# Turning the normalised context by a transposing DMA in place of TensorE transposes, in a fused gated cross-attention and FFN kernel

## What is computed

```
q_hk = (hidden_q @ Wq.T).reshape(Bv, Sv, H, K)
q_big = jnp.einsum('bshk,hkq->bshq', q_hk, w_kc_q)
...
q_r = jnp.einsum('bshq,hqr->bhsr', q_big, W_qr)
k_r = jnp.einsum('bld,hdr->bhlr', kv_r, W_kr)
scores = jnp.einsum('bhsr,bhlr->bhsl', q_r, k_r)
attn = jax.nn.softmax(scores, axis=-1)
ctx_c = jnp.einsum('bhsl,bld->bhsd', attn, kv_r)
ctx_lat = jnp.einsum('bhsd,hkd->bhsk', ctx_c, w_kc_kv)
ctx = ctx_lat.transpose(0, 2, 1, 3).reshape(Bv, Sv, H * K)
return ctx @ Wo.T
```

## Time and profile before

| | |
|---|---|
| median of 3 runs | 487.31 us (487.01 to 488.1) |
| the profiled execution | 489.46 us, its span 487.6 us |
| busy share PE / DVE / ACT / POOL | 86 / 77 / 58 / 53 % |
| stretch of the loop over the groups | about 142 to 345 us of the span |

### The profile page before, as it was taken

One profiled execution on the slowest core, in us unless ns is written; L12 is line 12 of the kernel. 1 busy time (PEld: TensorE's weight loads), 2 busy tenths in 40 slices (PEclk: granted clock), 3 DMA queues, 4 the chain that ended last, 5 costly groups with the idle time before them and its releaser, 6 DMA issues.

```text
span 487.6 us, 11500 instructions
## 1 busy us (share of the span) xinstructions
PE 418.3 (86%) x4416; PEld 313.0 (64%) x4416; DVE 377.1 (77%) x757; ACT 283.0 (58%) x640; POOL 257.7 (53%) x293
## 2 busy tenths in 40 slices
PE   2975898798967879989987898888879899999994
PEld 2445466346846756767665666666767678887773
DVE  4359998676668979886989999985765689888991
ACT  1677587775346666556655756646515456567660
POOL 3168131201345545546678777764353488888373
PEclk9997799999989999999999999987989999999998
DMA  8994003930124666668666745488211476777643
GB/s 258 268 340 105 0 2 99 367 125 1 60 69 92 129 108 131 121 105 146 113 111 149 138 80 85 78 184 177 52 47 54 116 194 174 190 174 214 192 50 34
DMA packets 104599, 62.60 MB, mean 128 GB/s; under 512 B 72032, under 2 KB 100704, under 8 KB 104352
## 3 DMA queue, kind: packets, MB, share of 16 engines
q1 hardware_dynamic: 99792, 56.69, 47.9%
q0 software_dynamic: 4224, 4.79, 5.8%
q10 hardware_dynamic: 528, 0.38, 0.4%
HBM read 40.27 MB, written 8.55 MB: 100 GB/s over the span
## 4 chain that ended last, share of the span: by engine, by line
PE 42%; DMA 16%; DVE 13%; ACT 10%; POOL 8%; issue 7%; SPq 1%; POOLq 0%; DVEq 0%; ACTq 0%
PE psum L2179 7%; DMA lw<-lw 6%; PE psum L1871 5%; PE psum L2195 4%; DMA y_sb<-lw 4%; DVE lw L1296 4%; ACT lw L965 3%; DMA out_x<-lw,tslot 3%; POOL out_x L753 3%; PE psum L1992 2%; PE psum L1796 2%; PE psum L1956 2%; DVE nmax L1353 2%; POOL lw L651 2%; PE psum L1938 2%
## 5 line engine op out<-in xcount | busy, mean ns | idle before, releaser
L651 POOL TENSOR_TENSOR lw<-lw 128x512 f32<-128x512 f32 x48 | 67.3, 1404 | 53.7 <-DVE lw L1296 53.6
L965 ACT ACTIVATE lw<-psum,nmax 128x256 f32<-128x256 f32 x128 | 59.0, 469 | 33.3 <-DVE nmax L1353 31.6
L1871 PE MATMUL psum<-lp 128*128 128x256 f16 x576 | 72.1, 276 | 0.0
L1296 DVE TENSOR_TENSOR lw<-psum,lp 128x1024 f32<-128x1024 f32 x48 | 58.4, 1218 | 7.8 <-PE psum L1871 6.8
L1871 PEld LDWEIGHTS psum<-lp 128*128 128x128 f16 x576 | 53.6, 99 | 14.0 <-issue 7.4
L1077 ACT ACTIVATE lw<-psum,b1w 128x320 f16<-128x320 f32 x64 | 33.7, 527 | 36.9 <-PE psum L2179 36.9
L2179 PE MATMUL psum<-lw,se 128*128 128x320 f16 x384 | 54.7, 299 | 0.0
L753 POOL DMA_INDIRECT out_x<-lw,tslot x24 | 43.8, 1827 | 18.2 <-DMA out_x<-lw,tslot 7.3
L972 ACT ACTIVATE lw<-lw 128x512 f16<-128x512 f32 x60 | 37.6, 630 | 27.0 <-DMA lw<-lw 19.8
L712 POOL TENSOR_TENSOR lw<-lw 128x512 f16<-128x512 f32 x30 | 35.6, 1187 | 30.8 <-ACT lw L972 30.8
L2179 PEld LDWEIGHTS psum<-lw,se 128*128 128x128 f16 x384 | 36.3, 97 | 16.6 <-DVE lw L1598 1.3
(11 more groups left out here) (248 smaller groups left out, 986.8 us busy)
## 6 DMA issues: line engine op xcount, KB each, us to landing
se<-in_w SPq DMA_DIRECT2D x11, 1024.0 KB
se<-in_w SPq DMA_DIRECT2D x40, 128.0 KB
dispatch<-in_empty SPq DMA_DIRECT2D x4, 662.5 KB, 9.3
lp<-in_Wq SPq DMA_DIRECT2D x2, 1024.0 KB, 9.7
se<-in_WoT SPq DMA_DIRECT2D x1, 2048.0 KB, 12.2
lw<-dispatch SPq DMA_DIRECT2D x7, 265.0 KB, 7.3
lp<-in_w_kc_q SPq DMA_DIRECT2D x2, 768.0 KB, 10.0
lp<-in_rotq SPq DMA_DIRECT2D x1, 1536.0 KB, 13.9
```

The source lines that it names most:

```text
L651: nc.gpsimd.tensor_tensor(rope[:, c % QT, :].rearrange("p (h s) -> p h s", h=2), straight, crossed[:, ::-1, :], ALU.add).then_inc(g_rope, 1)
L965: A_(e_sb[:, n % 2, st * S:(st + 1) * S], bank[3 + n % 2][:, st * S:(st + 1) * S], ACT.Exp, bias=nmax[:, n % 2, st:st + 1], accum_out=esum ...
L1296: V.tensor_tensor(t12[:, c % 2], tile_bank(c).unsqueeze(1).broadcast_to([P, 2, 2 * S]), rotq[:, c % QT], ALU.mult).then_inc(v_t1, 1)
L1871: ins = M(tile_bank(c)[:, half * S:(half + 1) * S], m1[w][:, kc, half, col:col + P], (yth, ytl)[a][:, kc, b * S:(b + 1) * S], start=(n == ...
```

## The change

For groups 0 to 13 the context is turned by SP's transposing DMA. ACT now writes the fp16 high half straight from `cxn` (`context_high`, at the place of `ct_high`), POOL the low half (`ct_low`, now on POOL), both into a free part of `y_sb`, and SP turns the two together into `ct` (`turned_context`). `project` waits for that DMA. PE's four transposes and DVE's subtraction go away for these groups; groups 14 and 15 keep the old way. Some semaphores of the routing steps are replaced by the wait chain `link`.

```diff
+NGD = NGB - 2
...
+            def turned_context(g):
+
+                sp.wait_ge(g_ct, g + 1)
+                if g >= 1:
+                    sp.wait_ge(p_out, g)
+                sp.dma_start_transpose(ct.rearrange("p w st a s -> p (w st a) s"), context_halves(g)).then_inc(d_ct, 16)
...
             for n in range(NHD):
                 turned_exps(n)
+                if n % G == 1 and n > G:
+                    turned_context(n // G - 1)
...
+            def ct_low(g):
+
+                pool.wait_ge(a_ct, g + 1)
+                halves = context_halves(g)
+                nc.gpsimd.tensor_tensor(halves[:, 512:1024], cxn, halves[:, 0:512], ALU.subtract).then_inc(g_ct, 1)
...
                 exps_low(n + 1)
+                if g >= 1:
+                    ct_low(g - 1)
                 if g + 2 < NGB:
                     rotate(QT * (g + 2))
                 exps_low(n + 3)
...
+            def context_high(g):
+
+                act.wait_ge(v_norm, g + 1)
+                if g >= 1:
+                    act.wait_ge(d_ct, 16 * g)
+                A_(context_halves(g)[:, 0:512], cxn, ACT.Copy).then_inc(a_ct, 1)
...
                 exps(n + 3)
                 if g >= 1:
-                    ct_high(g - 1)
+                    context_high(g - 1)
...
                 if g + 2 < NGB:
                     turn(QT * (g + 2) + 1)
-                if g >= 1:
-                    ct_low(g - 1)
...
             def project(g):
 
                 b = g // NG
-                pe.wait_ge(v_ct, g + 1)
+                if g < NGD:
+                    pe.wait_ge(d_ct, 16 * (g + 1))
+                else:
+                    pe.wait_ge(v_ct, g - NGD + 1)
...
                     queries(QT * (g + 2) + 1)
-                if g >= 1:
-                    turn_context(g - 1)
```

More of the change, by code:

```diff
@@ L158, in program @@
         cxn = w2([512])
-        ct = [w2([512], F16) for _ in range(2)]
+        ct = w2([1024], F16).rearrange("p (w st a s) -> p w st a s", w=2, st=TPB, a=2)
         nmax = sb("nmax", [P, 2, TPB])
@@ L302, in program @@
         s_y3, g_row, p_yT3, a_yT3, p_lg = sem("s_y3"), sem("g_row"), sem("p_yT3"), sem("a_yT3"), sem("p_lg")
-        g_nb, v_best, v_cnt, s_rows = sem("g_nb"), sem("v_best"), sem("v_cnt"), sem("s_rows")
-        v_sel, d_sel, s_base = sem("v_sel"), sem("d_sel"), sem("s_base")
+        g_nb, v_cnt, s_rows = sem("g_nb"), sem("v_cnt"), sem("s_rows")
+        v_sel, d_sel = sem("v_sel"), sem("d_sel")
+        g_ct, d_ct = sem("g_ct"), sem("d_ct")
         s_el, a_el, s_oh, p_pos, s_idx, v_meta = sem("s_el"), sem("a_el"), sem("s_oh"), sem("p_pos"), sem("s_idx"), sem("v_meta")
@@ L350, in turn_bank, with context_halves @@
             return (bank[5], bank[1])[n % 2]
+        def context_halves(g):
+            at = NT - 2 * TPB if g < (B - 1) * NG - 2 else 0
+            return y_sb[:, at:at + TPB, :].rearrange("p a b -> p (a b)").bitcast(F16)
         def context_bank(g):
@@ L978, in turned_high @@
                 A_(turned[n % 3][:, 0].rearrange("p st lt s -> p (st lt s)"), turn_bank(n)[:, :], ACT.Copy).then_inc(a_at, 1)
+            def context_high(g):
[3 more added lines that the diff above has]
+                A_(context_halves(g)[:, 0:512], cxn, ACT.Copy).then_inc(a_ct, 1)
             def ct_high(g):
-                act.wait_ge(p_ct, g + 1)
-                if g >= 1:
-                    act.wait_ge(p_out, g)
-                A_(ct[0], context_bank(g)[:, :], ACT.Copy).then_inc(a_ct, 1)
+                act.wait_ge(p_ct, g - NGD + 1)
+                act.wait_ge(p_out, g)
+                A_(ct[:, 0].rearrange("p st a s -> p (st a s)"), context_bank(g)[:, :], ACT.Copy).then_inc(a_ct, 1)
             def split_high(k):
@@ L1374, in norm @@
                 dve.wait_ge(p_cx, G * (g + 1))
-                if g >= 1:
-                    dve.wait_ge(p_ct, g)
+                if g > NGD:
+                    dve.wait_ge(p_ct, g - NGD)
+                elif g >= 1:
+                    dve.wait_ge(g_ct, g)
                 V.tensor_tensor(cxn.rearrange("p (a b) -> p a b", b=DC),
@@ L1382, in ct_low @@
                 dve.wait_ge(a_ct, g + 1)
-                V.tensor_tensor(ct[1], context_bank(g)[:, :], ct[0], ALU.subtract).then_inc(v_ct, 1)
+                high, low = [ct[:, w].rearrange("p st a s -> p (st a s)") for w in range(2)]
+                V.tensor_tensor(low, context_bank(g)[:, :], high, ALU.subtract).then_inc(v_ct, 1)
             def update(b):
@@ L1420, in route_best @@
                 for t, l in zip(ts, lg):
-                    V.max_index(i8[:, t, :], v8[:, t, :], l).then_inc(v_best, 1)
+                    ins = V.max_index(i8[:, t, :], v8[:, t, :], l)
+                link(ins)
             def route_choice(b):
                 ts = pair_of(b)
-                dve.wait_ge(v_best, TPB * (b + 1))
                 link(V.tensor_copy(idf[:, ts, :], i8[:, ts, 0:TOPK]))
@@ L1438, in route_sides @@
                                 ALU.subtract).then_inc(s_el, 1)
-                V.tensor_scalar(base[:, ts, :], idf[:, ts, :], float(CAP), spare[:, 0:1], ALU.mult, ALU.subtract)\
-                    .then_inc(s_base, 1)
+                link(V.tensor_scalar(base[:, ts, :], idf[:, ts, :], float(CAP), spare[:, 0:1], ALU.mult, ALU.subtract))
             def route_weights(b):
@@ L1475, in route_place @@
                 dve.wait_ge(v_cnt, 2 * b + 2)
-                dve.wait_ge(s_base, b + 1)
                 link(V.tensor_reduce(pos[:, ts, :], pr[:, ts, :, :], AX.X, ALU.add))
@@ L1923, in latent @@
                     pe.wait_ge(v_qz, g)
-                if g >= 3:
-                    pe.wait_ge(v_ct, g - 2)
                 x, y = bank[1], bank[2]
@@ L1999, in turn_context @@
                 pe.wait_ge(v_norm, g + 1)
-                pe.wait_ge(v_qz, min(g + 3, NGB))
+                pe.wait_ge(v_qz, NGB)
                 if g == NGB - 1:
@@ L2004, in turn_context @@
                     for pair in range(2):
-                        ins = TR(context_bank(g)[:, pair * S + st * P:pair * S + (st + 1) * P],
+                        ins = TR(context_bank(g)[:, (2 * st + pair) * P:(2 * st + pair + 1) * P],
                                  cxn[:, st * S + pair * P:st * S + (pair + 1) * P], identf[:, :])
@@ L2019, in project @@
                             last = g % NG == NG - 1 and pair == 1 and (a, w) == PASSES[-1]
-                            ins = M(bank[7][:, st * S:(st + 1) * S], ct[a][:, pair * S + st * P:pair * S + (st + 1) * P],
+                            ins = M(bank[7][:, st * S:(st + 1) * S], ct[:, a, st, pair, :],
                                     nn[w][:, 2 * (g % NG) + pair, :], start=(first and st == 0), stop=last,
@@ L2114, in select_rows @@
                     pe.wait_ge(v_t1, QT * NGB)
-                    pe.wait_ge(v_ct, NGB - 1)
+                    pe.wait_ge(v_ct, 1)
                 for t in (TPB * b, TPB * b + 1):
```

## The result

| | before | after |
|---|---|---|
| median | 487.16 us (4 runs) | 510.8 us (508.27 to 513.56, 4 runs) |
| ratio, 95% interval | | 1.0495 (1.0447 to 1.0544) |
| profiled execution, its span | 489.46, 487.6 us | 508.27, 506.5 us |

The changed kernel's lines are other ones: `project` is L2050, `context` L2019, `scores` L1983, `latent` L1958; on ACT `context_high` is L1009, `exps_high` L996; on POOL the new `ct_low` is L735, `rotate` L667, `exps_low` L728; on SP the context's DMA is L528, a head's DMA L484.

A forecast was written before the change was run, and what follows sets the result against it. No engine is full; a ring of waits through POOL's and SP's lists bounds the loop. Six passes at 1.5, four at 1.0 (4.0) and four at 0.4 (1.6) add 14.6 us to 487.31: 501.9 us, range 494 to 507.

The forecast's parts named there:

- Pass 4: Loop pass worked out by rows: SP issues the context, weight pieces and late heads 18 and 19; next `latent` +1.7 us.
- Passes 6, 10, 11, 12: Loop passes taken to be like pass 10, without weight pieces on SP; +1.0 us each, 4.0 together.
- Passes 5, 8, 9, 13: Loop passes taken to be like pass 5, with tight DVE or POOL's scatters; +0.4 us each, 1.6 together.
- first class: Loop passes 1, 2, 3, 4, 7, 14, like pass 4 with weight pieces on SP's list; +1.5 us each.
- last class: The same as Passes 5, 8, 9, 13: loop passes with tight DVE or POOL's scatters; +0.4 us each.
- The deeper one: Rival, 20%: `project` has its full delay in every pass, 14 x 1.9 = 26.6 us, 513.9; also covers a blocked port.
- The blocked port: Within the deeper rival: DVE and POOL operations reading SBUF lengthen each other when they meet, up to 1.1 us each.
- The faster one: Rival, 9%: PE's own list sets the passes, so its 9.2 us saving comes back nearly whole; 479.
- The hidden one: Rival, 5%: delays of heads n+2 and n+3 fall into idle time and PE's savings pay the rest; 487.3.
- The colder PE: Rival, 8%: longer gaps lower PE's granted clock; one 12 us slice at half clock costs about 10 us; 512.
- the 7 us that I had held ready: Upper allowance for the new DMA landing in 4.6 instead of 3.1 us in passes with high DMA share: 5 x 1.5.
- the ring: Loop's waits across engines taken to set each pass: DVE `turn`, POOL `rotate` and `exps_low`, head's DMA, PE `context`, next `latent`.

The follow-up runs named there:

- d3_spare_both: Kernel before plus an unused POOL subtraction and an unused transposing DMA waiting for it, at the change's places; 512.92 us, 1.0514.
- d4_both_behind: As d3_spare_both, with the spare DMA moved in SP's list from behind head n+1 to behind head n+3; 493.32 us, 1.0145.
- e4_high_early: The change with ACT's `context_high` moved ahead, right behind `qz_high` instead of behind head n+3's exponentials; 487.38 us, 1.0041 to before.
- f1_early_behind_piece: As e4_high_early, with the context's DMA behind head n+1's weight piece on SP instead of ahead of it; 489.53 us, 1.0071 to before.
- f2_early_first12: As e4_high_early, but groups 12 and 13 keep the old TensorE transposes; 486.92 us, 1.0020 to before.
- q1_not_turned: The change with turning of groups 0 to 13 left out (no transposes, low half or DMA), an incomplete computation; 483.42 us, 0.9945 to before.
- d2_spare_low: Kernel before with the change's `link` waits and an unused POOL subtraction at `ct_low`'s place, nobody waiting for it; 488.99 us, 1.0051.
- d1_spare_turn: Kernel before with the change's `link` waits and one unused transposing DMA per group on SP, waiting for nobody; 490.72 us, 1.0055.
- e1_project_late: The change with PE's `project` moved one pass later, behind the next pass's first queries; 523.98 us, 1.0764 to before.

## Why the prediction held, and where its sum was off

**The mechanism.** Heads n+2 and n+3 queued on SP behind a wait that passes through POOL to ACT: shown by d3_spare_both (1.0514 with nothing else of the change) and undone by either end, d4_both_behind (SP's order) and e4_high_early (ACT's).

**Pass 4.** Forecast +1.7 us, measured +2.36. Counted from each pass's own `latent`, `context_high` and its successors came 0.2 us later than worked out, gaps of 0.1 us between SP's issues another 0.2, and head 19 landed after 3.29 instead of 3.1 us.

**The sum.** From `latent` to `latent`, after less before: passes 1 to 4 and 7, forecast 1.5 each, measured 1.49 on average (2.41, -0.72, 1.78, 2.36, 1.61). Passes 6, 10, 11, 12, forecast 1.0, measured 1.45 (3.29, 2.57, 0.20, -0.27). Passes 5, 8, 9, 13, forecast 0.4, measured 1.32 (0.53, 2.09, 0.77, 1.89). The last is the term that was mis-sized most: 5.3 us in place of 1.6 (pass 14 was in the first class and ends outside the loop).

The 1.49 of the first class agrees by luck. Passes 3, 4 and 7, with the granted clock at 1.00 before and after, grew by 1.9 us on average, and pass 1 had a clock of 0.88 in place of 1.00. Against that stands pass 2: it takes 14.23 us before and 11.7 to 11.8 in e4_high_early, f1_early_behind_piece, f2_early_first12 and q1_not_turned. So the work taken away gives back some 2.5 us there, which the forecast did not have, and the delay ate 1.8 of it.

In the last class passes 5 and 9 came near the forecast, and 8 and 13 did not. I had taken DVE for the tight engine in all four, so that its own 0.68 us would pay. Pass 8 has a colder PE, below. In pass 13 SP issues two weight pieces behind each head and behind the context too; the change there:

```profile
340.96 1.24 SPq L528 DMA_TRANSPOSE lw<-y_sb  x1
342.26 1.05 SPq L473 DMA_DIRECT2D se<-in_w  x2
343.40 1.23 SPq L484 DMA_TRANSPOSE lw<-lw  x1
```

Head 54 is issued 11.3 us after the pass's `latent` at 332.07, where it was 8.9 before, and the pass grows by 1.9 us although its clock rose from 0.89 to 1.00: it is a pass like pass 4, and I had it in the wrong class. DVE is tight in none of them any more. Before, it was busy for 13.49 of pass 9's 14.57 us; after, by this row of the busy time, for 11.66 of 15.34:

```profile
275.37:290.71 15.34, 11.76 (x151) 8.82 (x148) 11.66 (x17) 8.22 (x24) 11.90 (x11) 1.00 0.80 170
```

**The clock.** The forecast had it only in a rival. Pass 6 before; pass 6 and pass 8 after; and a stretch of 4 us at the start of pass 6:

```profile
222.17:234.68 12.51, 12.14 (x160) 9.61 (x157) 9.98 (x20) 8.59 (x26) 7.63 (x9) 1.00 0.68 113
...
229.22:245.02 15.80, 13.51 (x155) 9.91 (x152) 11.26 (x22) 8.75 (x26) 9.35 (x10) 0.89 0.56 111
...
259.69:275.37 15.68, 12.57 (x147) 8.97 (x144) 11.79 (x13) 8.11 (x24) 10.59 (x11) 0.89 0.62 122
...
228.00:232.00 4.00, 3.23 (x32) 1.99 (x34) 1.57 (x4) 2.03 (x6) 1.74 (x4) 0.67 0.91 210
```

PE had been busy for 1.92 of the 4 us from 208, for 2.46 and 2.70 of two of the next three stretches, with a granted clock of 1.00; then 0.67 is a part at 1.2 GHz. `latent` of this pass, which the next steps wait for, took 3.8 us where it had taken 2.15 in pass 6 before at 1.00. So up to 1.65 of the pass's 3.3 us are clock. From pass 1 on the change has three such passes, 1, 6 and 8, and the kernel before one, 13. The four executions of the change took 508.27, 509.97, 511.63 and 513.56 us at a mean clock of 0.969, 0.949, 0.950 and 0.940.

So the forecast's 501.9 is low by 8.9 us. Of these, 4.2 are between its 504.1 for the profiled execution and the 508.27 measured, from the passes and the clock above; 2.2 are the distance by which the profiled execution of before lay above its median, which the forecast carried over; and 2.5 are the distance by which that of the change lay below its own, at the highest clock of the four.

**The rivals.** The deeper one had nearly the right time (513.9) and half of its rows: `project` does wait 1.8 us in every group. But the wait is not the cause: without it, d3_spare_both takes as long. It hides in the same delay: there PE stands at `context` instead, 21.6 us for heads to land (142 to 364 us), where it is 15.2 in the change and 12.1 before. That its time came near the measured one is luck. The blocked port is not seen: the mean of `exps_low` on DVE went from 850 to 742 ns and of `rotate` from 1404 to 1390 ns with one more POOL operation in a group, where the lock that I cited from the Trainium skill's "SBUF — State Buffer" would have them longer; with fewer DVE instructions in a longer pass they may meet less, but in d2_spare_low, with all of DVE's work, the means hardly moved either. The faster one is excluded by q1_not_turned: with PE's 9.2 us and DVE's 9.6 us gone, 2.7 us come back, so PE's own list does not set the passes. The hidden one is excluded by the result. The colder PE has the nearest time, 512, and its clock is there in passes 1, 6 and 8; but it comes on top of the delay in SP's list and not in its place, so its number too is right in part by luck.

**Costs beside the order.** The spare DMA by itself is 0.55% and the spare subtraction 0.51%, 5 us together, about twice what q1_not_turned gives back. The waits of `link`, which I had put at nothing, are in both and are not separated. The landing of the new DMA was like the others: median 3.1, at most 3.7 us, so nothing of the 7 us that I had held ready for it above. Two small slips in the forecast move no bound: 0.60 + 1.2 + 3.1 is 4.9 and not 4.95, and 5 x 1.5 is 7.5 and not 7.

**What stays open.** The share of the 24 us that is clock is not separated by a run. And why e4_high_early loses 1.6 us in pass 12 and 1.5 in pass 13 is half settled. f2_early_first12 has the old way from pass 13 on, for groups 12 and 13, and its pass 13 is as long as before (15.58 against 15.63 us), so the new way costs there. Its pass 12, still with the new way, is 1.5 us longer than before; but so is that of q1_not_turned, by 1.6, which issues no new DMA at all. So SP's list is not the cause in pass 12; what is stays open. Each of these is one profiled execution, and the median of f2_early_first12 is not below that of before.

## What to carry to other kernels

Before moving work to an in-order DMA queue, write down what stands behind it there and when its input is ready: a wait costs whatever is queued behind it, not what it waits for. If the place is given, make the source earlier; here one line on the producer was worth 22 us. And look for the ceiling first, by leaving the work out: 19 us of engine time taken off two busy engines were worth 2.7 us.

## What the runs showed of the hardware

- Transposing DMAs of 128 x 1024 fp16 that wait for no other engine cost a kernel that already issues 60 of them only 0.55% for 14 more (d1_spare_turn), though the DMA share of the loop rose from 0.65 to 0.76.
- The kernels with more waits on PE, of 1 to 3 us each, had the lower granted clock in the loop: 0.97 before, 0.95 in the change, 0.92 in d3_spare_both and, in e1_project_late, by its busy time of 142 to 380 us:

```profile
142.00:380.00 238.00, 187.23 (x2146) 138.72 (x2147) 160.39 (x248) 123.60 (x366) 139.40 (x138) 0.85 0.63 119
```

In e4_high_early, with most of `project`'s waits gone, it was back at 0.98. A delay on the ring can thus be paid twice: once as idle time, and again as slower matmuls on the same ring.
